# A fused graph-network kernel: the low half of a continuing state is made at the head of the next step, and side work and prologue are placed anew

## What is computed

```python
x = layernorm(x + L0(x, adj, W1, b1, W2, b2, fusion_w))
x = layernorm(x + L1(x, adj, nodemask, weight, w_ih, w_hh, b_ih, b_hh))

# L0: for each of five groups of the first 25 nodes, two normalized graph convolutions
#     (A + I, D^-1/2 on both sides), relu after each, weighted by softmax(fusion_w)[g], added to those nodes
# L1: a gated graph network with five layers
A = (adj != 0)
for l in range(5):
    m   = einsum('bnd,de->bne', h, weight[l])
    agg = einsum('bij,bid->bjd', A, m)
    h   = gru_cell(agg, h, w_ih, w_hh, b_ih, b_hh)     # r, z sigmoid; n tanh; (1-z)*n + z*h
out = h * mask
```

## Time and profile before

| | |
|---|---|
| median of 3 runs | 565.17 us (565.04 to 565.83) |
| the profiled execution: its time, its span | 564.52 us, 562.6 us |
| busy: TensorE, VectorE, ScalarE, GpSimd | 519.8 (92%), 447.4 (80%), 371.0 (66%), 259.5 (46%) us |
| mean granted clock of TensorE | 0.979 of full |
| share of the chain that ended last: TensorE, VectorE, GpSimd, ScalarE | 68%, 16%, 6%, 4% |

### The profile page before, as it was taken

How to read it: one execution, slowest core, us unless ns; L and a number is a source line. 1 busy time by engine, 2 the same in 40 slices (tenths; PEclk the granted TensorE clock), 3 DMA queues, 4 the chain that set the end, 5 groups by cost and what they waited for, 6 DMA issues and landing times.

```text
span 562.6 us, 8366 instructions
## 1 busy us (share of the span) xinstructions
PE 519.8 (92%) x2907; PEld 434.3 (77%) x2907; DVE 447.4 (80%) x970; ACT 371.0 (66%) x682; POOL 259.5 (46%) x304
## 2 busy tenths in 40 slices
PE   1969899999999999999999999999999999999980
PEld 1747788888778789887778788888878888888860
DVE  4268766779998877779998877779998899887785
ACT  2336665676586665777787666678787666788644
POOL 7275422673463225666373323566264324442335
PEclk9987999999999999999999999999999999999995
DMA  5839610000000000001000000000100000001002
GB/s 130 210 94 241 156 33 5 1 1 0 2 1 1 1 27 5 20 2 37 20 1 1 1 0 2 9 12 20 38 0 2 1 1 1 19 20 34 5 0 75
DMA packets 35664, 17.27 MB, mean 31 GB/s; under 512 B 4429, under 2 KB 35584, under 8 KB 35624
## 3 DMA queue, kind: packets, MB, share of 16 engines
q1 hardware_dynamic: 32569, 15.13, 10.3%
q10 hardware_dynamic: 2639, 1.42, 1.0%
q0 software_dynamic: 416, 0.20, 0.2%
HBM read 12.54 MB, written 4.19 MB: 30 GB/s over the span
## 4 chain that ended last, share of the span: by engine, by line
PE 68%; DVE 16%; POOL 6%; ACT 4%; issue 3%; ACTq 2%; DMA 1%; DVEq 0%; POOLq 0%
PE p L1065 14%; PE p L1067 14%; PE p L1066 14%; PE p L1059 9%; PE p L1052 6%; PE p L970 3%; DVE hT L802 2%; DVE cg L889 2%; DVE cg L892 2%; DVE xn L757 2%; DVE dg L800 2%; PE p L944 2%; PE p L963 1%; DMA rows<-in_L_gnn_b_hh_dram 1%; POOL dg L435 1%
## 5 line engine op out<-in xcount | busy, mean ns | idle before, releaser
L435 POOL TENSOR_TENSOR dg<-hT,ng 128x512 f32<-128x512 f32 x80 | 125.3, 1566 | 264.5 <-ACT ng L626 264.5
L1065 PE MATMUL p<-hhi,wh 128*128 128x512 f32 x240 | 102.9, 429 | 1.6 <-DVE cg L889 1.0
L889 DVE SCALAR_TENSOR_TENSOR cg<-p,biasc,rg 128x512 f32<-128x512 f32 x80 | 59.6, 744 | 55.1 <-ACT rg L613 54.8
L1065 PE MATMUL p<-ghi,wf 128*128 128x512 f32 x240 | 101.7, 424 | 0.0
L1066 PE MATMUL p<-hlo,wh 128*128 128x512 f32 x240 | 95.1, 396 | 0.0
L1067 PE MATMUL p<-hhi,wh 128*128 128x512 f32 x240 | 95.0, 396 | 0.0
L1067 PE MATMUL p<-ghi,wf 128*128 128x512 f32 x240 | 94.9, 395 | 0.0
L1066 PE MATMUL p<-glo,wf 128*128 128x512 f32 x240 | 94.9, 395 | 0.0
L788 DVE TENSOR_TENSOR hlo<-hT,hhi 128x512 fp32r<-128x512 f32 x76 | 75.8, 998 | 3.8 <-ACT hhi L637 0.6
L613 ACT ACTIVATE rg<-p,gb 128x512 f32<-128x512 f32 x80 | 55.3, 691 | 33.0 <-PE p L1067 27.0
L626 ACT ACTIVATE ng<-cg,biasc 128x512 f32<-128x512 f32 x80 | 57.9, 724 | 27.9 <-DVE cg L892 27.5
(11 more groups left out here) (129 smaller groups left out, 837.7 us busy)
## 6 DMA issues: line engine op xcount, KB each, us to landing
xn<-in_x_dram SPq DMA_DIRECT2D x8, 512.0 KB, 5.2
an<-in_adj_dram SPq DMA_DIRECT2D x8, 512.0 KB, 7.3
out_dram<-xn SPq DMA_DIRECT2D x16, 256.0 KB, 2.3
xt<-in_x_dram SPq DMA_DIRECT2D x16, 50.0 KB
w<-in_L_gnn_W_dram ACTq DMA_DIRECT2D x1, 640.0 KB, 8.8
w<-in_L_gnn_W_dram SPq DMA_DIRECT2D x1, 640.0 KB, 8.0
zg<-in_L_gnn_weight_dram ACTq DMA_DIRECT2D x1, 320.0 KB, 6.7
xt<-in_x_dram SPq DMA_DIRECT2D x8, 36.0 KB
```

The lines of the kernel that those rows point to most:

```text
L435: nc.gpsimd.tensor_tensor(dg[:, w.k % 2, :], hT[:, w.slot, :], ng[:, w.k % 2, :], ALU.subtract).then_inc(d_ok, 1)
L889: STT(cg[:, p, :], PH[:], bhn, rg[:, p, :], ALU.add, ALU.mult).then_inc(t1_ok, 1)
L1065: MM(bank[:], w[:, 0, cols], xhi, start=start, stop=False)
```

## The change

The low half of a state that goes on to another layer is made at the head of the following step, behind that step's side work and ahead of L889, rather than at the end of the step that made it; waits on `lo_ok` for the bank `PL` become waits on `hi_ok`. `scaled` goes behind `lo_neighbours`. The table gives the pieces of the graph convolution, its sums and the statistics other places. In the prologue, DMAs, transposes, copies and weight products are issued in another order, and some tiles are allocated in another order. The diff, cut to its core:

```diff
@@ class Plan
-    ADJ, Y, HA, HB, SA, SB, OA, OB, GATHER, BACK, REST = 2, 3, 4, 5, 6, 7, 8, 9, 10, 12, (13, 14)
-    DEGREES, SCALED, SPREAD = 11, 13, 14
-    ONES = {5: 0, 6: 1, 7: 2, 8: 3}
-    STATS1 = {14: 0, 15: 1, 16: 2, 17: 3}
-    APPLY1 = {15: [(0, 0)], 16: [(0, 1), (1, 0)], 17: [(1, 1), (2, 0)], 18: [(2, 1)], 19: [(3, 0)], 0: [(3, 1)]}
-    STATS2 = {4: 0, 6: 1, 8: 2, 10: 3}
-    APPLY2 = {7: [(0, 0), (0, 1)], 10: [(1, 0), (1, 1)], 11: [(2, 0)], 12: [(2, 1)], 13: [(3, 0)], 14: [(3, 1)]}
+    ADJ, Y, HA, HB, SA, SB, OA, OB, GATHER, BACK, REST = 2, 3, 4, 5, 6, 7, 7, 8, 9, 10, (12, 13)
+    DEGREES, SCALED, SPREAD = 8, 9, 10
+    ONES = {2: 0, 5: 1, 11: 2, 13: 3}
+    STATS1 = {11: 0, 14: 1, 15: 2, 16: 3}
+    APPLY1 = {12: [(0, 0)], 13: [(0, 1)], 15: [(1, 0)], 16: [(1, 1), (2, 0)], 17: [(2, 1), (3, 0)], 18: [(3, 1)]}
+    STATS2 = {3: 0, 4: 1, 6: 2, 7: 3}
+    APPLY2 = {4: [(0, 0)], 5: [(0, 1)], 6: [(1, 0)], 7: [(1, 1)], 9: [(2, 0), (2, 1)], 10: [(3, 0)], 11: [(3, 1)]}
...
@@ sync: the first chunk's rows
-            load_chunk(sp, 0)
             sp.wait_ge(ac_zero, 2)
             load_adj_rows(sp, 1, TB, ac_in[1])
+            load_chunk(sp, 0)
...
@@ gpsimd: prologue
             ones(0)
+            power(1)
             ones(1)
-            power(1)
+            deviation1(0)
             ones(2)
             ones(3)
-            deviation1(0)
             deviation1(1)
...
@@ scalar: DMAs
-            act.dma_start(wir, w_ih.rearrange("(c e) d -> e c d", c=3)).then_inc(gates_in, 16)
-            act.dma_start(whr, w_hh.rearrange("(c e) d -> e c d", c=3)).then_inc(gates_in, 16)
-            act.dma_start(wl, weight.rearrange("l c e -> c l e")).then_inc(wl_in, 16)
-            act.dma_start(w1[:], W1.rearrange("g d h -> d g h")).then_inc(w1_in, 16)
             for r0, src in ((0, b1.rearrange("g (c h) -> (g c) h", c=HC)), (NG * HC, b2),
...
                 act.dma_start(rows[r0:r0 + src.shape[0], :], src).then_inc(w_in, 16)
+            act.dma_start(wir, w_ih.rearrange("(c e) d -> e c d", c=3)).then_inc(gates_in, 16)
+            act.dma_start(whr, w_hh.rearrange("(c e) d -> e c d", c=3)).then_inc(gates_in, 16)
+            act.dma_start(w1[:], W1.rearrange("g d h -> d g h")).then_inc(w1_in, 16)
+            act.dma_start(wl, weight.rearrange("l c e -> c l e")).then_inc(wl_in, 16)
...
@@ vector: prologue, from the gathered sums on
             gather(0)
-            low_weights(0)
             add(0, True)
             norm1(0)
-            low_weights(1)
-            add(0, False)
+            for l in (2, 1, 0, 4):
+                low_weights(l)
             half_norm1(0, HALVES[1])
-            low_weights(2)
+            add(0, False, range(2))
+            lo_state(0, PL)
+            add(0, False, range(2, PACK))
+            lo_neighbours(0, PG)
             norm1(1)
-            low_weights(4)
-            lo_state(0, PL)
             low_weights(3)
-            lo_neighbours(0, PG)
...
@@ vector: the loop
-                if w.sg + 2 < CHUNKS and w.i == Plan.SCALED:
-                    scaled(w.sg + 2)
+                if k and ALL_WINDOWS[k - 1].turn == "step":
+                    lo_state(k + 2)
                 dve.wait_ge(r_ok, k + 1)
...
                 if w.feed:
                     lo_neighbours(k + 2, PG)
-                if w.turn == "step":
-                    lo_state(k + 3)
+                if w.sg + 2 < CHUNKS and w.i == Plan.SCALED:
+                    scaled(w.sg + 2)
...
@@ tensor: prologue
+            hidden_a(0)
+            hidden_b(0)
             pe.wait_ge(wl_in, 16)
+            pe.wait_ge(prep_lo, 1)
             for l in range(4):
                 last = TR(P[2][:, l * 128:(l + 1) * 128], wl[:, l, :], ident[:])
...
+            TR(P[1][:, GATES:512], wl[:, 4, :], ident[:]).then_inc(prep_t, 1)
             pe.wait_ge(w2_in, 16)
             second_a(0)
...
-            fused_weights(0)
             output_a(0)
             output_b(0)
-            fused_weights(1)
-            fused_weights(2)
-            pe.wait_ge(prep_a, 2)
+            pe.wait_ge(wlt_ok, 1)
+            for l in range(LAYERS):
+                fused_weights(l)
             back(0)
-            fused_weights(3)
-            fused_weights(4)
...
@@ tensor: the loop
                     if w.i == Plan.ADJ:
-                        pe.wait_ge(lo_ok, k + 2)
+                        if c == 1:
+                            pe.wait_ge(lo_ok, SLOTS)
+                        pe.wait_ge(hi_ok, k + 2)
                         pe.wait_ge(hT_ok, SLOTS * c)
...
                 if w.enter is not None and k >= 2:
                     pe.wait_ge(ob_ok, (NG - 1) * (w.enter // SLOTS + 1))
-                    pe.wait_ge(lo_ok, k + 2)
+                    pe.wait_ge(hi_ok, k + 2)
```

More of the change, by code:

```diff
@@ L134, in build @@
         an = sb("an", [128, B, N])
+        hT = sb("hT", [128, SLOTS, COLS])
+        hhi = sb("hhi", [128, SLOTS, COLS], f32r)
+        hlo = sb("hlo", [128, SLOTS, COLS], f32r)
+        nat = sb("nat", [128, SLOTS, SB, D])
+        ghi = sb("ghi", [128, SLOTS, COLS], f32r)
+        glo = sb("glo", [128, SLOTS, COLS], f32r)
+        rg = sb("rg", [128, 2, COLS])
+        zg = sb("zg", [128, 2, COLS])
+        cg = sb("cg", [128, 2, COLS])
+        ng = sb("ng", [128, 2, COLS])
+        dg = sb("dg", [128, 2, COLS])
+        wh = sb("wh", [128, 2, GATES], f32r)
+        wf = sb("wf", [128, LAYERS, 2, GATES], f32r)
         ident = sb("ident", [128, 128])
@@ L171, in build @@
         part = sb("part", [128, COLS_B])
[L173 to L184, removed]
         wir = rg[:, 0, 0:GATES].rearrange("p (c d) -> p c d", c=3)
@@ L564, in _ @@
             output_b(0)
-            for l in range(1, LAYERS):
+            for l in range(LAYERS):
                 high_weights(l)
@@ L837, in _ @@
             TT(fb2[:], biasc[:, NG * HC:BI], fw[:], ALU.mult).then_inc(b_ok, 1)
+            neighbours(0)
+            dve.wait_ge(prep_hi, 1)
+            TT(wh[:, 1, :], P[1][:, 0:GATES], wh[:, 0, :], ALU.subtract).then_inc(prep_lo, 1)
             hidden_b0(0)
@@ L916, in _ @@
             pe.wait_ge(ident_ok, 1)
-            pe.wait_ge(gates_in, 32)
-            for i in range(3):
-                last = TR(P[0][:, i * 128:(i + 1) * 128], wir[:, i, :], ident[:])
-            last.then_inc(prep_t, 1)
-            for i in range(3):
-                last = TR(P[1][:, i * 128:(i + 1) * 128], whr[:, i, :], ident[:])
-            last.then_inc(prep_t, 1)
             def fused_weights(l):
@@ L1018, in _ @@
             adjacency(0)
+            nr = NG * HC + NG + 6
+            pe.wait_ge(w_in, 16 * 4)
+            TR(P[3][:, 128:128 + nr], rows[:], ident[0:nr, 0:nr])
+            pe.wait_ge(mask_in, 16)
+            TR(P[3][:, 256:256 + B], maskr[:], ident[0:B, 0:B]).then_inc(prep_t, 1)
+            pe.wait_ge(gates_in, 32)
+            for i in range(3):
+                last = TR(P[0][:, i * 128:(i + 1) * 128], wir[:, i, :], ident[:])
+            last.then_inc(prep_t, 1)
+            for i in range(3):
+                last = TR(P[1][:, i * 128:(i + 1) * 128], whr[:, i, :], ident[:])
+            last.then_inc(prep_t, 1)
+            neighbours(0)
+            pe.wait_ge(w1_in, 16)
+            pe.wait_ge(wit_ok, 1)
+            pe.wait_ge(prep_a, 1)
+            hidden_a(0)
+            hidden_b(0)
             pe.wait_ge(wl_in, 16)
+            pe.wait_ge(prep_lo, 1)
             for l in range(4):
                 last = TR(P[2][:, l * 128:(l + 1) * 128], wl[:, l, :], ident[:])
-            last.then_inc(prep_t, 1)
-            TR(P[3][:, 0:128], wl[:, 4, :], ident[:]).then_inc(prep_t, 1)
-            nr = NG * HC + NG + 6
-            pe.wait_ge(w_in, 16 * 4)
-            pe.wait_ge(wlt_ok, 1)
-            TR(P[3][:, 128:128 + nr], rows[:], ident[0:nr, 0:nr]).then_inc(prep_t, 1)
-            neighbours(0)
-            pe.wait_ge(w1_in, 16)
-            hidden_a(0)
-            hidden_b(0)
+            TR(P[1][:, GATES:512], wl[:, 4, :], ident[:]).then_inc(prep_t, 1)
             pe.wait_ge(w2_in, 16)
             second_a(0)
-            pe.wait_ge(mask_in, 16)
-            pe.wait_ge(prep_a, 1)
-            TR(P[3][:, 256:256 + B], maskr[:], ident[0:B, 0:B]).then_inc(prep_t, 1)
             second_b1(0)
             second_b2(0)
-            pe.wait_ge(prep_lo, 1)
-            fused_weights(0)
             output_a(0)
             output_b(0)
-            fused_weights(1)
-            fused_weights(2)
-            pe.wait_ge(prep_a, 2)
+            pe.wait_ge(wlt_ok, 1)
+            for l in range(LAYERS):
+                fused_weights(l)
             back(0)
-            fused_weights(3)
-            fused_weights(4)
             def turn(bank, src):
@@ L1083, in _ @@
             pe.wait_ge(a_ok, 1)
-            pe.wait_ge(prep_lo, 4)
+            pe.wait_ge(prep_lo, 2)
             aggregate(0, PG, entering(0))
+            pe.wait_ge(prep_lo, 5)
             for w in ALL_WINDOWS:
```

39 lines of the change are left out of this document (15 added, 24 removed).

## The result

The changed kernel takes 557.62 us (median of 4 runs, 556.88 to 559.69) against 565.11 us (median of 4, 564.72 to 565.83): a ratio of 0.9872, 95% interval 0.9842 to 0.9902. The profiled execution took 557.08 us with a span of 554.8, 7.8 us less than before.

A forecast was written before the change was run, and what follows sets the result against it. The prediction took TensorE, busy 519.8 of 562.6 us, to bound the kernel. From 565.17 us it summed -10.27, -1.98, +0.6, +5.0, +3.5, -1.2, +0.4 and +1.0 to 562.2 us, range 558.4 to 565.4.

The forecast's parts named there:

- Tiles allocated elsewhere: The other order of tile allocation was taken to cost or gain nothing: 0 us.
- Statistics and sums regrouped: Places 10 to 19, chunks 0 to 2: VectorE no longer falls behind, the whole excess goes, -10.27 us.
- Rival (d): Collisions of VectorE and GpSimd, not the pile at place 14, make the excess; a third stays, 565.6 us; chance 0.08.
- The wait of ADJ: Adjacency transposes in chunks 1 and 2 wait for the rounded half, not the low half: -0.99 us twice, -1.98.
- GATHER to BACK: GpSimd's power precedes the additions, so TensorE waits at BACK: 2.4 us in chunks 0 and 1, 0.2 in 2; +5.0.
- Rival (a): BACK doesn't wait, GpSimd being busy 46% and ready in time: 557.2 us; chance 0.10.
- Hold +3.5: Step 0: the second slot's later statistics delay ScalarE's apply, and TensorE's transposes wait 3.5 us, between 3.0 and 3.9.
- Rival (b): Step 0 isn't held because the second slot comes in time; no hold, clock or give-back: 558.9 us; chance 0.09.
- Give-back -1.2: The 1.64 us wait of step 2 shrinks, as GpSimd's chain moves less than TensorE: -1.2 us, between 0 and -1.64.
- rival (c): Prologue: the port lock holds VectorE's half_norm1 in full beside the mask operation, 1.9 us for 0.4, 563.7; chance 0.09.
- The clock, +1.0: TensorE's granted clock falls to half around the wait in step 0: +1.0 us, between 0 and 2.2.
- Rival (e): The clock falls behind all three long waits, step 0 and BACK in chunks 0 and 1: 567.8 us, slower; chance 0.10.

The follow-up runs named there:

- b_aligned: The kernel before with two empty tiles, so that wh, wf and hT to dg begin on multiples of 128 bytes: 562.28 us, ratio 0.9951.
- a_off: The changed kernel with empty tiles that put hT to dg and wh, wf back on the old remainders, 32 and 96 bytes: 562.44 us, ratio 0.9958.
- A: The changed kernel itself, against the kernel before: 557.62 us, ratio 0.9872.
- a_lo_end: The changed kernel with the low half of a continuing state back at the end of the step that makes it: 561.05 us, ratio 0.9937.
- b_lo_head: b_aligned with the low half at the head of the step and the waits of ADJ on the rounded half: 555.50 us, ratio 0.9830.
- b_adj: b_aligned with only the waits of ADJ on the rounded half instead of the low half: 559.56 us, ratio 0.9910.
- a_power: The changed kernel with DEGREES, SCALED, SPREAD at places 9, 10, 12, so the power comes behind GATHER's additions: 556.08 us, ratio 0.9843.
- best: a_stats with DEGREES at 9, SCALED and SPREAD at 17, 18, later masks for slots 2 and 3, slot 0 applied one place later: 549.89 us, ratio 0.9739.
- a_stats: The changed kernel with slot 1's statistics ahead of glo of slot 0 in VectorE's prologue, behind all sums and the low half: 554.78 us, ratio 0.9820.
- b_loop: The changed kernel's loop and table behind the prologue of the kernel before, tiles on multiples of 128 bytes: 555.53 us, ratio 0.9832.
- b_loop_power: b_loop with the power of the degrees behind the additions, DEGREES, SCALED, SPREAD at 9, 10, 12: 554.05 us, ratio 0.9808.
- B: The kernel before the change: 565.11 us beside the changed kernel, 564.83 to 565.36 us beside the experiments.

## Why the prediction missed

*Tiles allocated elsewhere: 0.* This is the step that failed. `b_aligned` and `a_off` measured it, from both sides: 4.8 us in A. The diff showed it, and the trace of before couldn't have told its price, but it should have had a bound, since it touches the products of all 80 steps. The matmuls themselves start sooner after each other; no wait, overlap or path of the prediction is in it.

With the old remainders the sum gives 562.2 and `a_off` measures 562.4. That is partly luck: in its trace the first matmul of the loop comes 2.1 us sooner than the sum has it (44.54 for 46.23 + 0.4), and a fall of the clock in chunk 1, for which the sum has nothing there, takes 1.6 back. The other stretches agree within 0.4 us each.

*Statistics and sums regrouped, -10.27.* The size is nearly right, its reason only half. Places 10 to 19 of A are 5.8 us above clean steps (174.14 less three times 56.1), of which the waits at BACK are about 4.7 (2.2, 2.2 and 0.3, each step 10 against 5.92); so 1.1 of the excess is left, at places 13 and 14, behind the applying. But the prediction gave the head of the step nothing beyond the 0.3 us a step that it counted with the regrouping. Under the new table it is worth 2.1 us there (`a_lo_end`: 59.51, 59.35 and 57.41), under the old one 4.4 (`b_lo_head`), not quite half of the whole excess; the two overlap. Rival (d) has fallen in the form in which it was put, yet the collision that it named is in the sum: that is what the head avoids.

*The wait of ADJ, -1.98.* Right in kind; `b_adj` shows 1.25 and 1.22, and in A step 2 of chunks 1 and 2 is 6.22 for 7.46. The idle time of 0.99 understated it; where the rest lies was not looked into.

*OB one place earlier, +0.6.* Right: the step at place 9 is 5.74, against 5.48, and places 3 to 9 last 49.58 in A for 49.32 in `b_aligned`.

*GATHER to BACK, +5.0.* Measured 4.7, with the chain as worked out: power 2.24, additions 4.40 (4.75 was taken), transposes. Rival (a) has fallen. The chain was also what made it repairable: `a_power`, `best`.

*The start of the loop.* Hold +3.5: 3.13 of idle, and the place of the statistics is its cause (`a_stats`). Rival (b) has fallen. The first matmul came 1.43 us sooner, where 0 was taken and -0.8 was the bound; the start of the loop scatters from 44.5 to 46.2 us among the kernels that have this prologue, and from 45.3 to 47.1 among those with the old one, so about 1 us of it is the prologue's.

Give-back -1.2: -1.30 is measured, but it doesn't need the hold. `b_lo_head` and `b_loop`, without a hold, have step 2 at 6.79 and 6.77 us, and `b_loop_power`, with the same prologue as `b_loop`, at 8.10. What goes with it in all 18 profiles is VectorE's `hT` at the end of step 1. Before, it starts behind the start of GpSimd's next `dg` and takes 1.67:

```profile
60.03 1.45 POOL L435 TENSOR_TENSOR dg<-hT,ng 128x512 f32<-128x512 f32 x1 [0.42 <-ACT ng L626]
60.37 1.67 DVE L802 TENSOR_TENSOR hT<-ng,dg 128x512 f32<-128x512 f32 x1
```

and changed, ahead of it:

```profile
63.27 0.69 DVE L798 TENSOR_TENSOR hT<-ng,dg 128x512 f32<-128x512 f32 x1
63.47 1.65 POOL L434 TENSOR_TENSOR dg<-hT,ng 128x512 f32<-128x512 f32 x1 [3.02 <-ACT ng L622]
```

In four profiles (B, `b_aligned`, `b_adj`, `b_loop_power`) `hT` takes 1.67 to 1.76 and step 2 lasts 8.07 to 8.11 (in `b_adj`, where the clock fell behind it, 9.88); in the other fourteen it takes 0.69 and step 2 6.73 to 6.79. So the time comes or goes whole, and doesn't shrink by the share that a delay leaves over. With the new prologue it is gone in all twelve profiles; with the old one it can fall either way.

*half_norm1, +0.4.* Two instructions of 0.33 us became two of 0.46, so +0.26, though a mask operation had begun 0.10 ahead of them (41.13, theirs 41.23) and went on beside both; rival (c), the lock for 1.9 us, has fallen.

*The clock, +1.0.* Steps 0 and 1 are 4.83 longer with 3.13 of idle. That is not 1.7 for the clock: against `b_loop`, which has the same loop and no hold, they are 4.32 longer (17.98 for 13.66), which leaves 1.2, as `a_stats` does. The other 0.5 is the loop's own: `b_lo_head` has 13.55 for the 13.10 of `b_aligned`. Rival (e) is partly right: behind BACK's wait the clock fell in some executions. In the one shown of A it didn't; in `b_loop` it did in chunk 0 (windows; the wait ended at 121.37):

```profile
119.00:121.00 2.00, 0.33 (x2) 0.00 (x0) 0.81 (x3) 0.40 (x1) 1.56 (x4) 1.00 0.00 0
121.00:123.00 2.00, 1.63 (x9) 1.63 (x10) 0.74 (x3) 0.02 (x1) 1.54 (x2) 0.71 0.00 0
123.00:125.50 2.50, 2.50 (x7) 1.91 (x7) 1.51 (x4) 1.25 (x2) 0.00 (x0) 0.55 0.00 0
```

That step took 9.75 us for 8.12, so 1.6 us for a fall; the same in chunk 1 of `a_off` (9.73). A's runs scatter over 2.8 us, those of `best`, without waits at BACK, over 0.5. For the falls as the reason speaks that A's longest run (559.69) has the lowest mean granted clock, 0.974, and the others 0.979 to 0.980; it is not shown.

*The chances.* The parts that the prediction names add up to 0.11 for no change and 0.14 for slower, where it has 0.14 and 0.11; the 0.75 for faster is right.
